# Sums of squares in two stages: GpSimd folds the halves, VectorE sums the rest, and two pieces of work change their place

## The reference

```
q, k, v = split(shift(x) @ Wqkv)            # per head 64 columns
q = q / max(norm(q), 1e-12) * q_scale       # norm over the 64 columns of a head
k = k / max(norm(k), 1e-12) * k_scale
q = q * cos * scale + rotate_half(q) * sin * scale      # k likewise, with 1 / scale
out = softmax(mask(8 * q @ k.T)) @ v
```

## Time and profile before

| | before |
|---|---|
| median of 3 runs | 3413.21 us (3407.72 to 3415.92) |
| the profiled execution's own time | 3412.6 us |
| its span, first to last instruction | 3410.8 us |
| PE busy | 3286.0 us (96%) |
| DVE busy | 2796.2 us (82%) |
| ACT busy | 2299.8 us (67%) |
| POOL busy | 2259.8 us (66%) |

### The profile page before, as it was taken

One profiled execution on the slowest core, in us unless ns is written; L12 is line 12 of the kernel. 1 busy time (PEld: TensorE's weight loads), 2 busy tenths in 40 slices (PEclk: granted clock), 3 DMA queues, 4 the chain that ended last, 5 costly groups with the idle time before them and its releaser, 6 DMA issues. The chain is left out here.

```text
span 3410.8 us, 100964 instructions
## 1 busy us (share of the span) xinstructions
PE 3286.0 (96%) x42193; PEld 2145.6 (63%) x42193; DVE 2796.2 (82%) x4519; ACT 2299.8 (67%) x4541; POOL 2259.8 (66%) x1364
## 2 busy tenths in 40 slices
PE   8999699999999999999999999999999999999996
PEld 5555366666666666666666666666666666666663
DVE  2333698998988888989898889898999888988893
ACT  2222367777776777777777777777777777776774
POOL 0000377877777777777777777777777777777772
PEclk9999899999999999999999999999999999999998
DMA  2000001000001000001000010000010000000000
GB/s 73 1 1 1 4 11 36 11 11 11 8 17 36 10 10 11 11 16 34 11 11 11 8 42 11 11 9 11 11 42 8 11 11 11 12 13 17 15 8 13
DMA packets 62281, 52.50 MB, mean 15 GB/s; under 512 B 11526, under 2 KB 59396, under 8 KB 61828
## 3 DMA queue, kind: packets, MB, share of 16 engines
q1 hardware_dynamic: 61828, 46.05, 5.3%
HBM read 43.93 MB, written 2.10 MB: 13 GB/s over the span
## 5 line engine op out<-in xcount | busy, mean ns | idle before, releaser
L448 POOL TENSOR_TENSOR cosp<-cosp,rr 128x1024 f32<-128x1024 f32 x384 | 723.1, 1904 | 591.8 <-DVE rr L992 591.7
L458 POOL TENSOR_TENSOR cosp<-cosp,sinp 128x1024 f32<-128x1024 f32 x384 | 903.3, 2373 | 21.2 <-DVE sinp L971 21.2
L568 PE MATMUL ps<-w_qk,xs 128*128 128x512 f32 x1536 | 761.1, 618 | 24.1 <-ACT sq L776 19.7
L672 PEld LDWEIGHTS ps<-px,w_vo 128*128 128x128 f32 x6144 | 700.9, 192 | 54.1 <-ACT px L824 48.5
L672 PE MATMUL ps<-px,w_vo 128*128 128x128 f32 x6144 | 725.0, 276 | 3.1 <-ACT px L824 1.7
L776 ACT ACTIVATE sq<-ps 128x1024 f32<-128x1024 f32 x384 | 393.1, 1024 | 462.5 <-DVE sinp L971 462.5
L968 DVE TENSOR_TENSOR cosp<-ps,tab 128x1024 f32<-128x1024 f32 x384 | 469.3, 1222 | 110.7 <-PE ps L568 109.4
L568 PEld LDWEIGHTS ps<-w_qk,xs 128*128 128x128 f32 x1536 | 262.5, 190 | 387.2 <-issue 380.7
L977 DVE TENSOR_REDUCE ss<-sq 128x16 f32<-128x1024 f32 x384 | 455.4, 1186 | 57.5 <-ACT sq L776 57.2
L971 DVE TENSOR_TENSOR sinp<-ps,tab 128x1024 f32<-128x1024 f32 x384 | 466.3, 1214 | 0.0
L575 PEld LDWEIGHTS ps<-ident,cosp 128*128 128x128 f32 x3072 | 354.0, 142 | 117.0 <-DVE xb L1038 74.3
(11 more groups left out here) (107 smaller groups left out, 4437.3 us busy)
## 6 DMA issues: line engine op xcount, KB each, us to landing
tab<-in_tab SPq DMA_DIRECT2D x96, 128.0 KB, 2.1
qks<-in_scales SPq DMA_DIRECT2D x96, 128.0 KB, 3.4
w_qk<-in_L_ffn_Wqkv SPq DMA_DIRECT2D x12, 512.0 KB, 6.7
w_v<-in_wv_t SPq DMA_DIRECT2D x6, 512.0 KB, 8.2
w_o<-in_L_ffn_Wo SPq DMA_DIRECT2D x6, 512.0 KB, 9.3
x<-in_L_attn_x SPq DMA_DIRECT2D x16, 128.0 KB, 5.7
out<-w_v SPq DMA_DIRECT2D x16, 128.0 KB, 2.4
w<-in_L_ffn_W SPq DMA_DIRECT2D x6, 341.0 KB
```

Of the source, the lines that this page charges most:

```text
L448: eng.tensor_tensor(v, v, rr[:, B % 2, HEADS * i:HEADS * i + HEADS].unsqueeze(2).to_broadcast([P, HEADS, DH]), ALU.mult).then_inc(rot_read ...
L458: eng.tensor_tensor(cosp[:, A % 2, i, :], cosp[:, A % 2, i, :], sinp[:, i, :], ALU.add).then_inc(rot_added, 1)
L568: t = eng.matmul(ps[:, u, :], xs[:, n % ROUND, :], w_qk[:, n // TILES % 2, i, 512 * u:512 * u + 512], start=True, stop=True)
L672: t = eng.matmul(Y, w_vo[:, E // TILES % 2, i // HP, i % HP, :], px[:, i, :], start=i == 0, stop=i == HEADS - 1)
```

## The change

GpSimd gets two new instructions a step. `add_halves` takes the squares of q (or k), 16 heads of 64 columns, and adds the upper 32 columns of each head to the lower 32, in place; the one for q stands between L448 and L453, the one for k behind the two of L458. VectorE's sum then reads the lower 32 columns of each head only, and waits for GpSimd instead of ScalarE. Two places change with it: VectorE's sum for q goes from behind the reciprocal to behind the rope of k, and its sum for k from ahead of the maximum to behind it; ScalarE's guess goes from the end of a step to the next step, behind the three copies of the products with the tokens and ahead of the shift of the next input.

```diff
+            def add_halves(n, i):
+                eng.wait_ge(sq_done, 2 * n + i + 1)
+                v = sq[:, i, :].rearrange("p (h u f) -> p h u f", u=2, f=32)
+                eng.tensor_tensor(v[:, :, 0, :], v[:, :, 0, :], v[:, :, 1, :], ALU.add).then_inc(halves_done, 1)
...
                         eng.tensor_tensor(v, v, rr[:, B % 2, HEADS * i:HEADS * i + HEADS].unsqueeze(2).to_broadcast([P, HEADS, DH]),
                                           ALU.mult).then_inc(rot_ready, 1)
+                if tile(A):
+                    add_halves(A, 0)
                 if tile(C):
                     eng.wait_ge(recip_done, C + 1)
...
                         eng.tensor_tensor(cosp[:, A % 2, i, :], cosp[:, A % 2, i, :], sinp[:, i, :], ALU.add).then_inc(rot_added, 1)
+                if tile(A):
+                    add_halves(A, 1)
...
                         eng.copy(px[:, :, 32 * b:32 * b + 32], G(b).rearrange("p (h q) -> p h q", q=WIN)).then_inc(px_evac, 1)
+                T = turn_of(s - 1, 7)
+                if T is not None:
+                    eng.wait_ge(variance_done, 2 * T + 1)
+                if tile(B):
+                    eng.wait_ge(ssq_done, 2 * B + 2)
+                    after(eng, norm_step, normed(B))
+                    guess_roots(B, 0, 2 * HEADS + (TB if T is not None else 0))
+                elif T is not None:
+                    guess_roots(B, 2 * HEADS, 2 * HEADS + TB)
                 if tile(A + 1):
                     tile_input(A + 1)
...
-                T = turn_of(s, 7)
-                if T is not None:
-                    eng.wait_ge(variance_done, 2 * T + 1)
-                if tile(A):
-                    eng.wait_ge(ssq_done, 2 * A + 2)
-                    after(eng, norm_step, normed(s))
-                    guess_roots(s, 0, 2 * HEADS + (TB if T is not None else 0))
-                elif T is not None:
-                    guess_roots(s, 2 * HEADS, 2 * HEADS + TB)
...
             def square_sum(n, i):
-                eng.wait_ge(sq_done, 2 * n + i + 1)
+                eng.wait_ge(halves_done, 2 * n + i + 1)
                 if i == 0:
                     after(eng, norm_step, normed(n))
-                eng.tensor_reduce(ss[:, HEADS * i:HEADS * i + HEADS], sq[:, i, :].rearrange("p (h d) -> p h d", d=DH),
-                                  AX_X, ALU.add).then_inc(ssq_done, 1)
+                eng.tensor_reduce(ss[:, HEADS * i:HEADS * i + HEADS],
+                                  sq[:, i, :].rearrange("p (h u f) -> p h u f", u=2, f=32)[:, :, 0, :], AX_X, ALU.add).then_inc(ssq_done, 1)
...
-                if tile(A):
-                    square_sum(A, 0)
                 if tile(E):
...
                     rope(A, 1)
+                    square_sum(A, 0)
...
-                if tile(A):
-                    square_sum(A, 1)
                 if tile(B):
                     eng.wait_ge(sims_done, B + 1)
                     eng.tensor_reduce(mx[:, :], S, AX_X, ALU.max).then_inc(max_done, 1)
+                if tile(A):
+                    square_sum(A, 1)
```

More of the change, by code:

```diff
@@ L240, in build @@
         sq_done = sem("sq_done")
+        halves_done = sem("halves_done")
         ssq_done = sem("ssq_done")
```

## The result

The changed kernel takes 3590.65 us (median of 4 runs, 3585.94 to 3594.29) against 3414.57 us before (4 runs): ratio 1.0508, 95% interval [1.049, 1.0526]. The forecast was 3589. The profiled execution took 3593.92 us, its span 3592.1.

What follows compares the result with a forecast made beforehand. DVE and PE were taken to set the period before, a loop through POOL and DVE after: 189 steps of 16.32 us add 168.0, disturbed steps 7, the last tile about 1, +176 on 3412.6, so 3589 us (range 3465 to 3690).

Steps and rivals of the forecast that it cites:

- The loop: Roots, POOL's passes up to the halves of k, DVE's sum for k, px copy, subtraction, roots: 16.28 us a step; chance 0.70.
- Price of the passes: Each new POOL instruction was taken at 1.27 us, moving what follows by 1.23; bounds 0.95 and 2.37.
- the rival of dearer halves: POOL's new passes cost 1.90 us instead of 1.27, for operands with gaps: 3827 us; chance 0.12.
- the cheaper one: Rival: POOL's new passes cost 0.95 us each, mean step 15.68, 3475 us; chance 0.11.
- The half reduction: DVE's sum over the lower 32 columns of each head: 0.65 us, of which 0.56 count in a row.
- the handover from POOL to DVE: Time from the end of POOL's halves of k to DVE's sum for k: 0.08 us.
- Disturbed steps: 36 us of steps disturbed from outside the four-step pattern before; most swallowed, 7 left (bounds 0 and 36).
- the pattern's mean: Mean period over four kinds of step, from rope of q to rope of q: 15.24 us before, 16.32 forecast.
- The third rival: Not slower: the halves of k reach DVE before its maximum is done, the loop doesn't bind; 3379 us, chance 0.07.
- POOL's work behind the halves of k: At the end of POOL's step: at most 2.51 us, said to fit into 3.4 us until the next roots.
- D: Theory from later runs: a DVE instruction with two SBUF inputs does not get through while a POOL instruction runs.

## Why the prediction was right

- *The loop.* Every step of it is in the timelines above at its place: POOL's passes start 3.88 and 11.61 us behind the rope (worked out: 3.88 and 11.63), the halves of k end at 12.88 (12.90), the next rope comes at 16.25 (16.28). The kind that has the small POOL instruction in front takes 16.40 (16.44). The doubled pass shows that the loop bound every kind of step.
- *Price of the passes.* 1.267 us against 1.27 taken from the product of the same shape. The gaps of 32 columns cost nothing, so the rival of dearer halves falls, and the cheaper one too. The Trainium skill's rule on steps of more than 8 bytes ("GPSIMD Engine Reference", section "7. Performance pitfalls for Q7 kernels") speaks, as its wording has it, of the step between elements; the 1267 ns agree with that reading.
- *Two small errors that cancel.* The half reduction takes 0.68, 0.61 in a row, not 0.65 and 0.56; the handover from POOL to DVE takes 0.03 (612.81 to 612.84), not 0.08.
- *Disturbed steps.* From step 2 to step 191 the changed kernel takes 3096.3 us; 189 times the pattern's mean of 16.29 are 3078.8, so 17.5 stay, where I left 7: half of the 36 us is swallowed, not most of it. The forecast of 3091.5 for this stretch (168 + 7 above 2916.5) is 4.8 below it.
- *How much of the hit is luck.* The mechanism and the price of the pass are shown; that the total lies within 2 us is luck. The pattern's steps came out 5.7 us below the forecast in all (16.29 for 16.32), the disturbed ones 10.5 above it, and the four runs of the changed kernel alone spread over 8 us.
- *The third rival was priced wrongly.* I gave 3379 us for a loop that does not bind. With the loop open, by a whole sum for k or by the halves first without the gated products, it is 3488: I had worked out DVE's order alone. The late guess costs once the loop no longer hides it (16.06 and 15.77 in the two kinds that PE held at 15.63 and 15.50), and so does the sum for q behind the rope of k. Of the 180 us that the 189 steps lost, opening the loop by a whole sum for k gives back 104. The other 76 are what this order costs once the loop is open, nearly all of it by the places; they are no share of the changed kernel's loss, where the loop hides them.
- *A danger that I did not see.* I held that POOL's work behind the halves of k (2.51 us at most) fits into 3.4 us until the next roots. By my own sum 3.4 us reach to the next rope; the roots start at 15.28, 2.4 us behind the halves. It cost nothing even so, with nothing to spare. In step 16 of the changed kernel POOL's gated products end at 647.94, and DVE's first root instruction ends 0.08 behind that:

```profile
645.44 2.50 POOL L488 TENSOR_TENSOR hh<-aa,ge 128x512 f32<-128x512 f32 x2
```

```profile
646.71 1.22 DVE L1077 TENSOR_TENSOR sh<-ps,mx 128x1024 f32<-128x1024 f32 x1
647.84 0.18 DVE L994 SCALAR_TENSOR_TENSOR rhalf<-rguess 128x32 f32<-128x32 f32 x1
```

  The subtraction, with one input in PSUM, lies wholly beside POOL and keeps its time. The run with the halves first shows what it costs when the products end 1.9 us behind the start of the roots (643.34 and 641.45).
- Not shown: how long the roots would take with an input in PSUM, the remedy that D suggests; the kernel uses all eight banks of `ps`, so it was not tried.

## What to carry to other kernels

Before work is given to an engine with idle time, look at what ends that idle time and what the new work's reader feeds: if the chain from the reader leads back to what the engine waits for, the idle time is part of a loop. Once that loop is the longest chain of a step, more work in it lengthens every turn by its full duration, as the doubled pass did. Write the loop down as a sum of starts to starts; here that gave the period to 0.03 us. When an order is changed, compare durations as well as starts: short VectorE instructions that suddenly last as long as a GpSimd instruction beside them are not slow but shut out.

## What the runs showed of the hardware that was not expected

A VectorE instruction with both inputs in SBUF (128x32, 0.19 us) lasts until the GpSimd instruction beside it ends: 1.27 us beside a pass of 1.27, 0.59 beside a copy of 0.61, 1.20 beside a product of 1.27. Over all the runs 516 root instructions take 0.3 us or more, and each ends 0.04 to 0.09 us behind the end of a GpSimd instruction; none ends while a GpSimd instruction that started ahead of it still runs. Between two GpSimd instructions in a row one gets through (642.16 above). A two-input and a one-input GpSimd instruction do it alike; VectorE instructions with one input in PSUM, or with a single input in SBUF, kept their time. GpSimd instructions that read nothing were not tried. The Trainium skill says that GpSimd shares its SBUF interfaces with VectorE and contends with VectorE instructions that have two SBUF inputs ("GPSIMD Engine Reference", section "8. Key points"). The runs agree, and give the size: not a slower rate but a wait to the end of the GpSimd instruction.
